# Five stages of a twelve-block decoder ordered by due times, and the scans' time step on GpSimd

## What is computed

```python
x = x + _L0_attn_ref(_layernorm(x), ...)    # product-key memory attention
x = x + _L0_xattn_ref(ctx, ctx, _layernorm(x), ...)
x = x + _L0_ffn_ref(_layernorm(x), ...)     # 32 experts, top 4, and shared ones
x = x + _L1_attn_ref(_layernorm(x), ...)    # mamba
x = x + _L1_xattn_ref(ctx, mask, _layernorm(x), ...)
x = x + _L1_ffn_ref(_layernorm(x), ...)
x = x + _L2_attn_ref(_layernorm(x), ...)
x = x + _L2_xattn_ref(_layernorm(x), ctx, ...)
x = x + _L2_ffn_ref(_layernorm(x), ...)     # 8 experts, top 1
x = x + _L3_attn_ref(_layernorm(x), ...)    # a second state-space model
x = x + _L3_xattn_ref(_layernorm(x), ctx, ...)
x = x + _L3_ffn_ref(_layernorm(x), ...)     # dense layer with LoRA experts, top 2
```

```python
Delta = jax.nn.softplus(...)
A_bar = jnp.exp(-Delta[..., None] * A)
BX = (Delta * h)[..., None] * Bm[:, :, None, :]
_, states = jax.lax.associative_scan(comb, (A_bar, BX), axis=1)
y = jnp.einsum('blfn,bln->blf', states, Cm) + D * h
```

## Time and profile before

| quantity | value |
|---|---|
| time, median of 3 runs | 4128.17 us (4126.56 to 4131.38) |
| the profiled execution, its own time | 4137.42 us |
| its span in the profile | 4135.9 us |
| PE busy / mean granted clock | 3217.4 us (78%) / 0.87 of full speed |
| DVE / ACT / POOL busy | 2401.6 / 1643.8 / 1412.9 us (58% / 40% / 34%) |
| DMA | 116.36 MB, mean 28 GB/s |

### The profile page before, as it was taken

The page is one execution under the profiler, slowest core; times in us unless marked ns, Lnnn a source line. Parts: engine busy times, 40 slices in busy tenths (PEclk is TensorE's granted clock), DMA queues, the critical chain, the costliest instruction groups (busy, mean ns, idle before and its releaser), DMA issues. The chain is left out here.

```text
span 4135.9 us, 53041 instructions
## 1 busy us (share of the span) xinstructions
PE 3217.4 (78%) x17661; PEld 2052.2 (50%) x17661; DVE 2401.6 (58%) x6477; ACT 1643.8 (40%) x3713; POOL 1412.9 (34%) x1086
## 2 busy tenths in 40 slices
PE   5888888676890678777699999478779677768898
PEld 3666666554660223322466666345656423325655
DVE  6787887247333799999343443534542258875543
ACT  3566665111120455454244444415602144436511
POOL 3666666210436254555222222301010135540110
PEclk7888888788995799999899999788969878889999
DMA  2000000300444000000000000011121200000000
GB/s 95 5 7 9 6 9 6 138 11 13 118 114 134 17 0 0 0 0 0 16 8 1 1 1 1 11 50 64 40 81 32 59 22 1 0 29 2 2 1 21
DMA packets 71175, 116.36 MB, mean 28 GB/s; under 512 B 28704, under 2 KB 58552, under 8 KB 68160
## 3 DMA queue, kind: packets, MB, share of 16 engines
q1 hardware_dynamic: 61312, 86.76, 6.2%
q0 software_dynamic: 9600, 26.23, 2.6%
HBM read 88.84 MB, written 24.12 MB: 27 GB/s over the span
## 5 line engine op out<-in xcount | busy, mean ns | idle before, releaser
L1210 POOL TENSOR_TENSOR L_attn_state<-L_attn_state,L_attn_ccol 128x1024 f32<-128x1024 f32 x192 | 458.4, 2389 | 456.1 <-DVE L_attn_state L1203 353.4
L1168 PE MATMUL bank<-L_attn_state,ident 128*128 128x512 f32 x768 | 416.2, 668 | 107.3 <-POOL L_attn_state L1210 72.4
L1203 DVE TENSOR_TENSOR_SCAN L_attn_state<-L_attn_decay,bank 128x1024 f32<-128x1024 f32 x192 | 438.6, 2284 | 22.7 <-ACT L_attn_decay L1179 3.5
L1179 ACT ACTIVATE L_attn_decay<-L_attn_dt,L_attn_A 128x512 f32<-128x512 f32 x384 | 256.2, 716 | 206.3 <-DVE L_attn_state L1203 163.3
L1168 PEld LDWEIGHTS bank<-L_attn_state,ident 128*128 128x128 f32 x768 | 152.1, 210 | 279.6 <-issue 123.6
L1107 POOL TENSOR_TENSOR L_xattn_prob<-L_xattn_prob,L_xattn_inv 128x1024 f32<-128x1024 f32 x64 | 121.1, 1893 | 411.9 <-DVE L_xattn_inv L1090 411.9
L1195 DVE TENSOR_TENSOR bank<-L_attn_dtx,bank 128x1024 f32<-128x1024 f32 x192 | 235.6, 1227 | 28.9 <-PE bank L1162 23.7
L1162 PE MATMUL bank<-L_attn_parts,L_attn_select 96*128 96x512 bf16 x384 | 145.4, 418 | 126.7 <-DVE bank L1195 110.1
L1185 ACT COPY L_attn_ccol<-bank 128x512 f32<-128x512 f32 x192 | 110.8, 577 | 208.4 <-PE bank L1162 191.5
L2813 POOL TENSOR_TENSOR L_attn_t<-L_attn_t,L_attn_base 128x1024 f32<-128x1024 f32 x96 | 183.2, 1909 | 21.6 <-DVE L_attn_base L2762 21.6
L1162 PEld LDWEIGHTS bank<-L_attn_parts,L_attn_select 96*128 96x128 bf16 x384 | 38.2, 104 | 291.1 <-DVE bank L1195 178.2
(11 more groups left out here) (599 smaller groups left out, 7551.0 us busy)
## 6 DMA issues: line engine op xcount, KB each, us to landing
L_ffn_ew<-in_L_ffn_experts SPq DMA_DIRECT2D x4, 3072.0 KB, 21.2
L_ffn_made<-L_ffn_yout SPq DMA_DIRECT2D x24, 512.0 KB, 3.0
L_ffn_w<-in_L_ffn_w SPq DMA_DIRECT2D x4, 2048.0 KB, 14.6
L_xattn_ctx<-in_ctx_rows SPq DMA_DIRECT2D x3, 2048.0 KB, 8.7
L_ffn_rows<-L_ffn_xh SPq DMA_DIRECT2D x8, 512.0 KB, 2.9
L_ffn_made<-L_ffn_yout SPq DMA_DIRECT2D x12, 256.0 KB, 2.1
L_attn_rows<-in_x SPq DMA_DIRECT2D x16, 128.0 KB, 6.8
turned<-L_attn_rows SPq DMA_DIRECT2D x16, 128.0 KB, 2.3
```

Source lines behind the costliest of these rows:

```text
L1168: t = pe.matmul(self.y[unit % len(self.y)][m][:, :], self.c.ident[:, :], self.state[N % 3][:, m, :], start=n == 0, stop=n == 15)
L1179: t = act.activation(self.decay[N % 2][:, m, :], dt[:, m, :], ACT.Exp, scale=A[:, m, n:n + 1])
L1203: dve.tensor_tensor_scan(flat(self.state[N % 3]), flat(self.decay[N % 2]), flat(self.drive), 0.0, ALU.mult, ALU.add).then_inc(*self.scanne ...
L1210: pool.tensor_tensor(state[:, :, :], state[:, :, :], self.ccol[N % 2][:, :].unsqueeze(1).broadcast_to([P, 2, GT]), ALU.mult).then_inc(*sel ...
```

## The change

Six stages get other orders. Memory attention, both routings and LoRA take due tables in place of orders by hand; steps that held work of several engines are split by engine (`turn`/`turned`, `gate`/`sigmoid` or `logits`, `shared_up`/`silu`/`lift`, and so on), so that each part has a due time of its own. Both scans get new numbers, and their time step leaves VectorE: GpSimd does the sum as `step`, and the product with x and the memset as `strength`, which from the third group (mamba) or unit on also waits until the last `drive` of the buffer's former use has been read. LoRA's `h1` gets two buffers. `top1` runs 23 tiles in place of 24 (8 experts over 2048 tokens need at most 16 + 7), and writes the last one alone.

```diff
-MAMBA_BY_UNIT = {"finish": 17.89}
+MAMBA_BY_UNIT = {"finish": 17.2}
...
-                  "step": (-1.84, 2.37), "out": (35.35, 37.03), "add": (36.41, 38.1)}
+                  "step": (-2.94, 3.25), "strength": (-1.85, 3.6), "out": (35.97, 37.51), "add": (36.34, 38.48)}
...
-        elif what == "step":
-            g, half = divmod(n, 2)
-            now, by = halves(dt[g % 2], half), halves(dtx[g % 2], half)
-            dve.wait_ge(*placed.at(n))
-            dve.tensor_tensor(now, now, halves(soft, half), ALU.add).then_inc(*mixed.up())
-            dve.wait_ge(*mixed.at(n, 0))
-            dve.wait_ge(*silued.at(g))
-            dve.tensor_tensor(by, now, halves(xc[g % 2], half), ALU.mult).then_inc(*mixed.up())
-            dve.wait_ge(*mixed.at(n, 1))
-            dve.memset(now.rearrange("p m (b t) -> p (m b) t", b=GROUP)[:, :, 0:1], LONG).then_inc(*driven.up())
...
+        elif what == "step":
+            g, half = divmod(n, 2)
+            now = halves(dt[g % 2], half)
+            pool.wait_ge(*placed.at(n))
+            pool.tensor_tensor(now, now, halves(soft, half), ALU.add).then_inc(*mixed.up())
+        elif what == "strength":
+            g, half = divmod(n, 2)
+            now, by = halves(dt[g % 2], half), halves(dtx[g % 2], half)
+            pool.wait_ge(*mixed.at(n, 0))
+            pool.wait_ge(*silued.at(g))
+            if g >= 2:
+                pool.wait_ge(*scan.brow.emptied(16 * (2 * (g - 2) + half) + 15))
+            pool.tensor_tensor(by, now, halves(xc[g % 2], half), ALU.mult).then_inc(*mixed.up())
+            pool.wait_ge(*mixed.at(n, 1))
+            pool.memset(now.rearrange("p m (b t) -> p (m b) t", b=GROUP)[:, :, 0:1], LONG).then_inc(*driven.up())
...
-        elif what == "step":
-            now = dt[n % 2]
-            dve.wait_ge(*placed.at(n))
-            dve.tensor_tensor(now[:, :, :], now[:, :, :], soft[:, :, :], ALU.add).then_inc(*mixed.up())
-            dve.wait_ge(*mixed.at(n, 0))
-            dve.tensor_tensor(dtx[n % 2][:, :, :], now[:, :, :], h[n % 2][:, :, :], ALU.mult).then_inc(*mixed.up())
-            dve.wait_ge(*mixed.at(n, 1))
-            dve.memset(now[:, :, :].rearrange("p m (b t) -> p (m b) t", b=GROUP)[:, :, 0:1], LONG).then_inc(*driven.up())
...
+        elif what == "step":
+            now = dt[n % 2]
+            pool.wait_ge(*placed.at(n))
+            pool.tensor_tensor(now[:, :, :], now[:, :, :], soft[:, :, :], ALU.add).then_inc(*mixed.up())
+        elif what == "strength":
+            now = dt[n % 2]
+            pool.wait_ge(*mixed.at(n, 0))
+            if n >= 2:
+                pool.wait_ge(*scan.brow.emptied(16 * (n - 2) + 15))
+            pool.tensor_tensor(dtx[n % 2][:, :, :], now[:, :, :], h[n % 2][:, :, :], ALU.mult).then_inc(*mixed.up())
+            pool.wait_ge(*mixed.at(n, 1))
+            pool.memset(now[:, :, :].rearrange("p m (b t) -> p (m b) t", b=GROUP)[:, :, 0:1], LONG).then_inc(*driven.up())
...
+LORA_BY_GROUP = {"root": -11.65, "stats": -11.01, "norm": -10.84, "turned": (-8.79, -7.89), "turn": (-7.92, -7.03), "logits": -7.82, "choose": -7.11,
+                 "weigh": -7.06, "shift": -6.92, "gate": -6.45, "masked": -5.12, "down": -4.01, "flipped": (-3.3, -1.98), "flip": (-2.23, -1.48),
+                 "up": (-0.86, 1.09, 2.5, 3.04, 3.91, 4.05, 7.46, 8.3), "relu": (-0.68, 1.15, 1.2, 2.49, 4.13, 7.01, 7.89, 8.47),
+                 "add": (-0.12, 0.46, 1.08, 3.47, 4.05, 5.58, 6.15, 8.66), "out": (9.27, 12.19), "outed": (11.22, 12.32)}
...
-    h1, h2 = s.sb("h1", [P, FC, GT]), [s.sb(f"h2{n}", [P, GT]) for n in range(3)]
+    h1, h2 = [s.sb(f"h1{n}", [P, FC, GT]) for n in range(2)], [s.sb(f"h2{n}", [P, GT]) for n in range(3)]
...
-            for m in range(FC):
-                yield "up", FC * g + m
-                if ahead:
-                    yield ahead.pop(0)
-                if m:
-                    yield "add", FC * g + m - 1
-            yield "add", FC * g + FC - 1
-            if ahead:
-                yield ahead.pop(0)
-            yield "out", 2 * g
-            if ahead:
-                yield ahead.pop(0)
-            yield "out", 2 * g + 1
+        yield from as_due(due_by(LORA_BY_GROUP, 10, range(NGROUP)))
...
-            if g and m == 0:
-                act.wait_ge(*out.filled(2 * g - 1))
+            if g >= 2 and m == 0:
+                act.wait_ge(*out.filled(2 * (g - 2) + 1))
...
+BY_UNIT = {"score": -0.87, "scopy": 0.32, "top": 0.35, "raise": 0.75, "shift": 0.93, "total": 1.06, "spare": 1.15, "base": 1.24, "log": 1.4,
+           "pick": 1.73, "exp": 1.96, "turn": 2.1, "recall": 2.48, "tcopy": 2.66, "keep": 3.3, "rcopy": 3.55}
+BY_BLOCK = {"xturn": -6.43, "norm": -5.99, "xcopy": -5.4, "qsum": -3.59, "square": -3.4, "scale": -3.17, "qmul": -3.06, "out": 12.98, "y": 13.45,
+            "ynorm": 14.61, "store": 14.84}
+BY_HALF = {"query": (-5.65, -3.93), "qadd": (-4.64, -3.76), "qturn": (-2.92, -2.69), "qcopy": (-2.53, -0.82), "pair": (8.53, 9.32),
+           "sm": (9.18, 9.42), "mix": (9.59, 10.53), "oT": (10.38, 12.85), "den": (10.65, 12.66)}
...
-            if n + 1 < UNITS:
-                if (n + 1) % chunks == 0:
-                    yield from ahead
-                    ahead = []
-                yield "score", n + 1
-            if n == 0:
-                yield from begins
-            if 0 <= n - 2 < UNITS:
-                yield "exp", n - 2
-            if 0 <= n - 1 < UNITS:
-                yield "log", n - 1
-            if 0 <= n - 5 < UNITS:
-                yield "rcopy", n - 5
...
-            if 0 <= n - 1 < UNITS:
-                yield "base", n - 1
...
+        due = [(n + at, key, n) for key, at in BY_UNIT.items() for n in range(UNITS)]
+        due += [(chunks * a + at, key, a) for key, at in BY_BLOCK.items() for a in range(NSEQ)]
+        due += [(chunks * a + at, key, 2 * a + half) for key, both in BY_HALF.items() for a in range(NSEQ) for half, at in enumerate(both)]
...
+ONE_BY_GROUP = {"stats": -2.74, "norm": -2, "turn": (-1.67, -1.09), "root": -1.62, "turned": (-0.76, -0.76), "logits": -0.67, "gate": -0.38,
+                "choose": -0.28, "flip": 0.23, "flipped": 0.31, "owe": (0.82, 0.86), "owed": (0.91, 1.24), "hold": 4.02}
...
-def top1(c, s, w, name, experts=8, ff=1024, tiles=24):
+def top1(c, s, w, name, experts=8, ff=1024, tiles=23):
...
-            yield "turn", 2 * g
-            yield "turn", 2 * g + 1
-            yield "gate", g
-            yield "choose", g
-            yield "flip", g
-            yield "owe", 2 * g
-            yield "owe", 2 * g + 1
+        yield from routing()
...
-        elif what == "down" and n % 2:
+        elif what == "down" and (n % 2 or n == tiles - 1):
...
+FOUR_BY_GROUP = {"root": -5.55, "stats": -1.69, "norm": -1.21, "turn": (-1.07, -0.95), "turned": (-0.84, -0.61), "gate": -0.64, "sigmoid": -0.58,
+                 "silu": (-0.56, 0.05), "shared_up": (-0.29, -0.2), "choose": -0.2, "lift": (0.14, 0.17), "shared_down": (0.3, 0.59),
+                 "lower": (0.52, 1.02), "hold": 1.12}
...
-            yield "shared_up", 2 * g
-            yield "shared_up", 2 * g + 1
-            yield "choose", g
-            if g + 1 < NGROUP:
-                yield "norm", g + 1
-                if g + 2 < NGROUP:
-                    yield "stats", g + 2
-            yield "shared_down", 2 * g
-            yield "shared_down", 2 * g + 1
...
-        elif what == "shared_down":
-            g, half = divmod(n, 2)
-            if half == 0:
-                dve.wait_ge(*norm.normed.at(g))
-                for j in range(2):
-                    dve.wait_ge(*side.filled(side["shared_up", 2 * g + j]))
-                    dve.wait_ge(*side.emptied(side["shared_gate", 2 * g + j]))
...
+        elif what == "lift":
+            at = side["shared_up", n]
+            dve.wait_ge(*side.filled(at))
+            dve.wait_ge(*side.emptied(side["shared_gate", n]))
+            dve.tensor_tensor(hS[n % 2][:, :], hS[n % 2][:, :], side.bank(at)[:, :], ALU.mult).then_inc(*side.done(at))
+        elif what == "lower":
+            at = side["shared_down", n]
+            if n % 2 == 0:
```

207 lines of the change are left out of this document (77 added, 130 removed).

## The result

The changed kernel takes 3923.07 us (median of 4 runs, 3919.26 to 3925.78), the kernel before in the same runs 4129.77 us. The ratio is 0.9499, with a 95% interval of 0.9483 to 0.9516: 5% faster, and 83 us faster than the forecast of 4006.

What follows compares the result with a forecast made beforehand. The prediction took no single engine as the bound, but in each stage the wait that ends last, with VectorE full in mamba. Terms -30 -18 -14 -8 -16 -18 -18 = -122 us gave a forecast of 4006 us, range 3945 to 4075.

Steps and rivals of the forecast that it cites:

- Memory, -30 forecast: Memory attention: VectorE wins 2.0 us per block over 15 blocks as its wait for the logarithm goes; TensorE's waits only shrink.
- the bound of -84: Memory attention: most that could be won, all 5.6 us of TensorE's two waits per block gone 15 times.
- Top-4, -18: Top-4 routing: next group's turns and gates overlap this group's `shared_down`; three periods fall from 24.4 to 18.4 us.
- top-1, -14 and -8: Top-1 layer: three routing periods fall from 16.2 to 11.5 us, -14; one tile of 7.85 us goes, -8.
- Mamba, -16: Mamba scan: 26.2 us leave VectorE, less 10 us of stall from GpSimd's two inserted operations per half.
- the stall of 10: Mamba: GpSimd's second insertion makes scans wait 1.25 us per half, eight times, +10 us.
- Sequence SSM, -18: `sequence_ssm`: -16 us for products and sums off VectorE, -6 for its waits for TensorE, +4 for GpSimd's insertions.
- LoRA, -18: LoRA: three of TensorE's four waits for the last sum into `h1` go, 13.4 us, plus 5 us from the clock.
- B: Whole kernel: more is won, through a higher TensorE clock in the routings and both memory waits lost; 3965 us, chance 0.17.
- A: Scans and memory stage: they return nothing, 4070 us, or one of the three pays, about 4050, the value taken; chance 0.22.
- D: Whole kernel: the order does not change where time goes, the scan core's sequence being the same; 4120 us, chance 0.06.
- C: Scans and memory stage: GpSimd becomes the late engine and the kernel gets slower, 4158 us; chance 0.05.

Runs made afterwards that it cites:

- fillers: The kernel before with eight, then fourteen, transposes of the identity ahead of each of TensorE's two memory-stage waits per block: 4102.12 and 4097.49 us.

## Why the prediction was wrong

The direction held, and five of the terms came near; the term for memory was wrong, and it alone put the time outside the range. Of the five, three came near by luck in part: `top1`, `mamba` and `sequence_ssm` below.

**Memory, -30 forecast, -102.5 measured: the step that failed.** It read "TensorE's two waits are only made smaller", and took only "the 2.0 us per block that VectorE wins". Both waits went whole, and the 2.0 us alone are worth nothing: with `base` early in the old order the period rose by 1.2. I had compared due times (the pair products 0.23 units behind the last `keep`, the query's turn 0.14 behind its product) as if they were times of the run; they only sort the steps. What decides is what stands between the two on the waiting engine's own queue: here the pair products, 1.2 us, in front of the query's turn, and 1.8 us of `recall` in front of the pair products. (The list of signs even has the wait for `keep` gone, 2.3 us per block, more than the 2.0 of the sum. And 38.4 and 5.6 are 44.0, not the period of 43.1: the two come from different stretches.) Second, VectorE's 4.6 us per block at L2779 stood in the same rows and were left out of the sum: they end when TensorE's wait ends. Third, TensorE's 38.4 us of work per block were taken as a floor. They were not: 300 to 348 us before the change held 9 us at the lower clock, behind and around its waits (in 315 to 318 and 324 to 327 us TensorE has under 1.1 us of work):

```profile
315.00:318.00 3.00, 0.75 (x6) 0.42 (x4) 2.90 (x13) 2.97 (x10) 2.84 (x5) 1.00 0.03 6
318.00:321.00 3.00, 2.05 (x12) 1.58 (x12) 3.00 (x23) 0.58 (x2) 3.00 (x2) 0.84 0.34 81
321.00:324.00 3.00, 3.00 (x13) 1.94 (x12) 1.69 (x6) 2.10 (x4) 1.83 (x2) 0.50 0.00 0
324.00:327.00 3.00, 1.00 (x10) 0.89 (x10) 0.25 (x1) 1.95 (x5) 2.43 (x3) 0.50 0.00 0
327.00:330.00 3.00, 2.94 (x20) 2.34 (x20) 1.70 (x8) 0.67 (x2) 0.92 (x1) 0.50 0.00 0
330.00:333.00 3.00, 3.00 (x34) 2.52 (x33) 2.90 (x22) 1.51 (x3) 1.27 (x1) 0.96 0.04 8
```

With the waits gone the same products take 33.9 us per block. The period of 37.0 is below my "floor", and the bound of -84, made from the waits only, was no bound. The clock's part is 1.4 to 2.2 of the 6.1 us; the rest is the order. The two kernels that put a wait of TensorE back into the new order lost 4.0 and 10.6 us, so its waits carry most of it, and the place of `base` is needed with them. The two parts don't add up exactly, since fillers also take time, and what each due time is worth alone is not defined: `base` early is worth -9.1 in the new order and +1.2 in the old, where it only made VectorE wait longer for the pair products.

**Top-4, -18 against -17.2; top-1, -14 and -8 against -19.1.** The period of `top4` came out as said (18.3). In `top1` the tile gave 8.2, and the three shorter periods 15.3; the first choice starts 2.5 us later in the stage (8.9 against 6.4 us after its start). In all the routing became 10.9 us shorter, where 14 was forecast, and the tiles 8.2, which is the 19.1. That the mean period is 11.1, where 11.5 was said, is luck: the 11.5 were TensorE's 10.7 us of work per group and a little more, but two of the three periods are about 8.0 and the third holds the wait of 9.8 us for the row write, which was not seen. With the loads split all three are near 7.8 and the routing takes 59.8 us. So TensorE's work per group bounds the routing as a whole and not the distance between two choices, since parts of it can stand before the first or behind the last.

**Mamba, -16 against -26.4.** The 26.2 us off VectorE are right; the stall of 10 is not. No scan waits for a sum. Behind GpSimd's insertions a `weigh` starts up to 3.7 us after its scan, as I had worked out, but from the end of that scan to the start of the scan three later lie 8.8 to 12.8 us in the trace where I had 8.25, since VectorE does other work in between at these places; at least 1.9 us are left. That the sum then came so near the measured value is luck in part: with the old tables the move gave only 14.4. Nor was the price of the product on VectorE constant: its median is 3.25 us there with the new tables.

**Sequence SSM, -18 against -19.1: right for the wrong reason.** I gave 16 to the move; it gives nothing, and the order gives 21.5. VectorE wasn't full there, as the prediction said, and the conclusion should have been drawn.

**LoRA, -18 against -22.2.** Three of the four waits went, 13.4 us, and TensorE's busy time fell by 8.8 us where I had 5 for the clock. That the second buffer makes it possible was wrong: with one buffer some 16 of the 22 us are left.

**Rivals.** B, more than the sum, is what came, at 0.17. Its far end, 3923, is the measured time to the microsecond, and that is chance: memory gave 18.5 us more than its -84, which was built from the waits alone, while the 15 us for a higher clock in `top1`'s routing did not come (granted 0.53 there, 0.50 before; 0.80 in `top4`'s, 0.81 before), and `mamba` gave 26.4 for its 30. A is out: the memory stage alone gave 101 us. D is out by the same run. C is out by GpSimd's rows: VectorE waits for GpSimd's step only at the first `drive`, 10.7 us at `mamba`'s start (5.7 before, for ScalarE) and 8.0 at the other scan's. What A says of moving work between VectorE and GpSimd, that it might not help, held in `sequence_ssm` (+2.4 us) and not in `mamba` (-28.5).

## What to carry to other kernels

Where an engine runs in order, count its wait by what stands behind it: here 3.9 us of wait on TensorE went with 4.0 us more of period, and 1.6 us more of busy time with 0.3. Before taking an engine's busy time as a floor, look at its clock in short windows behind its waits, and bound the gain with the work at the full clock. A due time has a worth only inside its order (0.21 of a unit was 9 us per block here), so undo such a change one number at a time from the new side, not from the old.

## What was not expected of the hardware

Fourteen transposes of a constant, thrown away, in each of TensorE's two waits per block made the old kernel faster by 0.7% (0.9903 to 0.9956), with the granted clock at 0.99 in place of 0.86. In `mamba` with the new tables the product of two tiles of SBUF took 1.22 us on VectorE at best and 3.25 in the median, where it met GpSimd's `weigh`, while the same operation took 2.37 on GpSimd in the median: the slower engine was the cheaper place.
